# Second attention: one bank and one exponential per transposed score tile, four banks for the other scores, values twice per unit

## What is computed

```python
q = q.reshape(Bx, Sx, N_GROUPS, R, HEAD_DIM).transpose(0, 2, 3, 1, 4)
k = k.reshape(Bx, Sx, N_GROUPS, HEAD_DIM).transpose(0, 2, 1, 3)
v = v.reshape(Bx, Sx, N_GROUPS, HEAD_DIM).transpose(0, 2, 1, 3)
sim = jnp.einsum('bgrsd,bgtd->bgrst', q, k) / math.sqrt(HEAD_DIM)
attn = jax.nn.softmax(sim, axis=-1)
out = jnp.einsum('bgrst,bgtd->bgrsd', attn, v)
```

## Time and profile before

| | |
|---|---|
| median of the runs | 1134.88 us |
| the profiled execution | 1137.65 us, of which the span from first to last instruction is 1135.8 us |
| TensorE (PE) busy | 1015.3 us, 89% |
| VectorE (DVE) busy | 758.1 us, 67% |
| ScalarE (ACT) busy | 592.0 us, 52% |
| stretch of the second attention's units | about 478 to 922 us of the span |

### The profile page before, as it was taken

The page is one execution under the profiler, slowest core; times in us unless marked ns, Lnnn a source line. Parts: engine busy times, 40 slices in busy tenths (PEclk is TensorE's granted clock), DMA queues, the critical chain, the costliest instruction groups (busy, mean ns, idle before and its releaser), DMA issues.

```text
span 1135.8 us, 17286 instructions
## 1 busy us (share of the span) xinstructions
PE 1015.3 (89%) x5701; PEld 744.4 (66%) x5701; DVE 758.1 (67%) x1575; ACT 592.0 (52%) x894; POOL 317.3 (28%) x330
## 2 busy tenths in 40 slices
PE   4999897769999927799998999999999987999996
PEld 3877776669999913555554555555555565888885
DVE  6576544465665436799889888888888846443438
ACT  6324544265555542466665666566656565444431
POOL 2005777065664410000000122222221000455342
PEclk9999999789999969799999999999999998999998
DMA  6862333354444272021121222222222115333244
GB/s 232 326 263 114 112 118 123 104 185 136 132 127 136 98 309 45 7 34 29 26 31 25 44 53 59 58 59 49 64 56 43 63 48 175 107 100 108 89 164 179
DMA packets 48962, 120.20 MB, mean 106 GB/s; under 512 B 7736, under 2 KB 24760, under 8 KB 48344
## 3 DMA queue, kind: packets, MB, share of 16 engines
q1 hardware_dynamic: 35968, 82.67, 25.3%
q0 software_dynamic: 11760, 32.24, 7.5%
q10 hardware_dynamic: 1152, 4.19, 0.9%
HBM read 72.17 MB, written 52.29 MB: 110 GB/s over the span
## 4 chain that ended last, share of the span: by engine, by line
PE 66%; DVE 14%; POOL 7%; ACT 4%; issue 4%; DMA 4%; SPq 0%; ACTq 0%; DVEq 0%; POOLq 0%
PE psum L827 10%; PE psum L849 10%; PE psum L836 8%; POOL xg L475 5%; PE psum L642 5%; PE psum L643 4%; PE psum L644 4%; DVE work_f L1726 4%; PE psum L556 4%; PE psum L557 3%; PE psum L558 3%; PE psum L628 3%; PE psum L653 2%; DVE x L1326 1%; ACT work_f L1219 1%
## 5 line engine op out<-in xcount | busy, mean ns | idle before, releaser
L1726 DVE TENSOR_REDUCE work_f<-psum 128x1 f32<-128x512 f32 x512 | 334.7, 684 | 51.0 <-PE psum L827 49.5
L1219 ACT ACTIVATE work_f<-psum 128x1024 f32<-128x1024 f32 x172 | 168.9, 1023 | 111.9 <-PE psum L836 108.6
L827 PE MATMUL psum<-work_r 128*128 128x512 f32 x512 | 205.0, 439 | 19.9 <-DVE work_f L1726 6.8
L482 POOL DMA_INDIRECT yk<-yb,dest x133 | 129.9, 977 | 241.9 <-ACT yb L1072 213.1
L827 PEld LDWEIGHTS psum<-work_r 128*128 128x128 f32 x512 | 94.2, 190 | 131.3 <-DVE work_f L1726 75.2
L836 PE MATMUL psum<-qm,work_r 128*128 128x512 f32 x512 | 161.9, 398 | 4.2 <-ACT work_f L1219 2.7
L475 POOL DMA_INDIRECT xg<-xn,slot x112 | 108.1, 966 | 180.4 <-PE psum L865 152.2
L836 PEld LDWEIGHTS psum<-qm,work_r 128*128 128x128 f32 x512 | 93.6, 188 | 31.8 <-ACT work_f L1219 10.9
L1219 ACT ACTIVATE pt<-psum 128x1024 f32<-128x1024 f32 x84 | 82.8, 1023 | 50.2 <-PE psum L836 47.6
L642 PE MATMUL psum<-wexp,xbh 128*128 x266 | 103.0, 387 | 6.5 <-issue 5.4
L643 PE MATMUL psum<-wexp,xbh 128*128 x266 | 96.9, 364 | 0.0
(11 more groups left out here) (218 smaller groups left out, 2044.7 us busy)
## 6 DMA issues: line engine op xcount, KB each, us to landing
xb<-xg SPq DMA_DIRECT2D x66, 258.0 KB
xg<-in_pad SPq DMA_DIRECT2D x1, 10320.0 KB
yg<-yk SPq DMA_DIRECT2D x20, 512.0 KB, 9.5
stage<-in_moe SPq DMA_DIRECT2D x16, 608.0 KB
xg<-in_pad SPq DMA_DIRECT2D x1, 7224.0 KB
work_r<-work_r SPq DMA_DIRECT2D x128, 48.0 KB
work_r<-work_r SPq DMA_DIRECT2D x32, 192.0 KB
stage<-in_moe SPq DMA_DIRECT2D x16, 384.0 KB, 3.8
```

What stands on the lines that cost most here:

```text
L482: nc.gpsimd.indirect_dma_start(yk[l], bass.IndirectOffsetOnAxis(ap=dest[:, j % 8, i:i + 1], axis=0), yb[l][:, j % 2, i, :], None).then_inc ...
L827: nc.tensor.matmul(next_bank(pe, ("scores", n), b_mx, n + 1), qs[g % 2][:, t * P:(t + 1) * P], km[g % 4][:, r, :], start=True, stop=True). ...
L1219: nc.scalar.activation(pt[((b * NG + g) * QT + t) % 3][:, 2 * h:2 * h + 2, :], psum[:, 3 + 2 * h:5 + 2 * h, :], ACT.Exp, scale=float(HD) * ...
L1726: v.reduce_max(mx[:, s % 2, i:i + 1], ring["scores", n], AX.X).then_inc(b_mx, 1)
```

## The change

The ring grows to four banks from the 17th use on (banks 3, 2, 0, 1 in turn), so each use waits for the reader of the use four before. The transposed scores get banks 4, 5 and 6, one tile each, and tile m waits for the exponential of tile m-3. ScalarE takes 16 exponentials of 128x512 per unit in place of 8 of 128x1024. The tables put the transposed scores at steps 5 to 16, in ones and twos, and the value tiles two and two at steps 12 and 18, instead of two, one and one at 15, 19 and 25. At step 2 the value tiles now come ahead of the maxima's transposes. The outputs' transposes move from step 11 to 10, the projections from 13 to 8, the values' transposes from 12 to 8; ScalarE's part of `compact` moves from behind the sixth of 8 exponentials to behind the sixth of 16, and its copy of bank 7 to the head of a unit's exponentials.

```diff
-            return {"maxima": 2, "outputs": 11, "values": 12 if s == NG + 1 else never,
-                    "project": 13 if following and NG - 3 <= s < NG else never}
+            return {"maxima": 2, "outputs": 10, "values": 8 if s == NG + 1 else never,
+                    "project": 8 if following and NG - 3 <= s < NG else never}
...
-        ring, read = {}, []
+        ring, holder, uses = {}, {3: (b_va, 1)}, []
 
         def next_bank(engine, use, reader, value):
-            if len(read) >= 3:
-                engine.wait_ge(*read[-3])
-            ring[use] = psum[:, (len(read) + 1) % 3, :]
-            read.append((reader, value))
+            n = len(uses)
+            bank = (n + 1) % 3 if n < QT * R else (3, 2, 0, 1)[n % 4]
+            if bank in holder:
+                engine.wait_ge(*holder[bank])
+            ring[use] = psum[:, bank, :]
+            holder[bank] = (reader, value)
+            uses.append(bank)
             return ring[use]
+
+        def transposed_bank(m):
+            return psum[:, 4 + m % 3, :]
...
             def scores_t(b, g, i):
...
-                t, h = i // 2, i % 2
-                if g >= 1 or i >= 2:
-                    pe.wait_ge(b_ex, b * (2 * NQ) + (g * 2 * QT + i - 1))
-                for r in (2 * h, 2 * h + 1):
-                    ins = nc.tensor.matmul(psum[:, 3 + 2 * h + r % 2, :], km[g % 4][:, r, t * P:(t + 1) * P],
-                                           qm[g % 2], start=True, stop=True)
-                ins.then_inc(b_st, 1)
+                t, r = i // R, i % R
+                m = b * NP + g * QT * R + i
+                if m >= 3:
+                    pe.wait_ge(b_ex, m - 2)
+                nc.tensor.matmul(transposed_bank(m), km[g % 4][:, r, t * P:(t + 1) * P],
+                                 qm[g % 2], start=True, stop=True).then_inc(b_st, 1)
...
-            TRANSPOSED = (4, 5, 8, 11, 12, 13, 16, 17)
-            VALUED = (15, 15, 19, 25)
+            TRANSPOSED = (5, 6, 6, 7, 8, 8, 9, 10, 11, 12, 13, 13, 14, 15, 15, 16)
+            VALUED = (12, 12, 18, 18)
...
-                    if i == turn["maxima"] and back:
-                        maxima_t(b, s - 1)
                     if i == TRANSPOSED[0] and back:
 
                         pe.wait_ge(b_qm, b * NG + s)
                     if s >= 2:
                         follow(b, s - 2, QT * R + i)
+                    if i == turn["maxima"] and back:
+                        maxima_t(b, s - 1)
...
-                        for h in range(2):
-                            if s >= 2 and s % 2 and (t, h) == (1, 1):
+                        tile = (b * NG + s - 1) * QT + t
+                        for r in range(R):
+                            if s >= 2 and s % 2 and (t, r) == (0, 0):
                                 outputs(b, s - 2)
...
+                            if (t, r) == (1, 2) and following and NG - 3 <= s < NG:
+                                compact((0, 2, 1)[s - (NG - 3)], b + 1, ring["projection", b * 3 + s - (NG - 3) + 4], s - (NG - 3))
+                            act.wait_ge(b_st, tile * R + r + 1)
+                            if tile >= 3:
+                                act.wait_ge(b_pv, tile - 2)
+                            nc.scalar.activation(pt[tile % 3][:, r, :], transposed_bank(tile * R + r),
                                                  ACT.Exp, scale=float(HD) ** -0.5).then_inc(b_ex, 1)
-                    if t == 2 and following and NG - 3 <= s < NG:
-                        compact((0, 2, 1)[s - (NG - 3)], b + 1, ring["projection", b * 3 + s - (NG - 3) + 4], s - (NG - 3))
```

More of the change, by code:

```diff
@@ L384, in stack_keys @@
                 else:
-                    sp.wait_ge(b_st, 2 * QT * (u - 3))
+                    sp.wait_ge(b_st, QT * R * (u - 3))
                 for r in range(R):
@@ L806, in _ @@
             pe.wait_ge(m_y, pairs(0, NPAIR[0]))
-            NP, NQ = NG * QT * R, NG * QT
+            NP = NG * QT * R
             def project(n, b1, o):
@@ L830, in scores_t @@
             def scores_t(b, g, i):
-                t, h = i // 2, i % 2
-                if g >= 1 or i >= 2:
-                    pe.wait_ge(b_ex, b * (2 * NQ) + (g * 2 * QT + i - 1))
-                for r in (2 * h, 2 * h + 1):
-                    ins = nc.tensor.matmul(psum[:, 3 + 2 * h + r % 2, :], km[g % 4][:, r, t * P:(t + 1) * P],
-                                           qm[g % 2], start=True, stop=True)
-                ins.then_inc(b_st, 1)
+                t, r = i // R, i % R
[4 more added lines that the diff above has]
+                                 qm[g % 2], start=True, stop=True).then_inc(b_st, 1)
             def values(b, g, t):
-                pe.wait_ge(b_ex, b * (2 * NQ) + ((g * QT + t) * 2 + 2))
+                pe.wait_ge(b_ex, b * NP + (g * QT + t + 1) * R)
                 n = b * NG + g
@@ L866, in maxima_t @@
                 ins.then_inc(b_mt, 1)
-            TRANSPOSED = (4, 5, 8, 11, 12, 13, 16, 17)
-            VALUED = (15, 15, 19, 25)
+            TRANSPOSED = (5, 6, 6, 7, 8, 8, 9, 10, 11, 12, 13, 13, 14, 15, 15, 16)
+            VALUED = (12, 12, 18, 18)
             def follow(b, g, step):
-                for n in range(2 * QT):
+                for n in range(QT * R):
                     if TRANSPOSED[n] == step:
@@ L1211, in stage @@
                     if back:
-                        g = s - 1
-                        for h in range(2):
-                            if s >= 2 and s % 2 and (t, h) == (1, 1):
+                        tile = (b * NG + s - 1) * QT + t
+                        for r in range(R):
+                            if s >= 2 and s % 2 and (t, r) == (0, 0):
                                 outputs(b, s - 2)
[L1216 to L1219, removed]
+                            if (t, r) == (1, 2) and following and NG - 3 <= s < NG:
[4 more added lines that the diff above has]
+                            nc.scalar.activation(pt[tile % 3][:, r, :], transposed_bank(tile * R + r),
                                                  ACT.Exp, scale=float(HD) ** -0.5).then_inc(b_ex, 1)
-                    if t == 2 and following and NG - 3 <= s < NG:
-                        compact((0, 2, 1)[s - (NG - 3)], b + 1, ring["projection", b * 3 + s - (NG - 3) + 4], s - (NG - 3))
                 if last and s == NG:
```

## The result

The changed kernel takes **1145.34 us** (median of 4 runs, 1144.6 to 1146.13), the kernel before 1134.84 us over the same runs: ratio 1.0097, 95% interval 1.0082 to 1.0112, so 9.3 to 12.7 us slower. The forecast was 1136.4 with a range of 1126 to 1149 and "a draw leaning to slower". The profiled execution of the changed kernel took 1146.13 us with a span of 1144.3, 8.5 more than the span before. The profiled execution before lay 2.8 us above its median and this one 0.8, which is why the medians differ by 10.5.

What follows compares the result with a forecast made beforehand. TensorE's streaming time plus stalls was taken to bound each second-attention unit. Plain -1.5, outputs -3.0, projections +8.0, values' transposes -2.6, head -2.3 and tail +2.9 gave +1.5 us on 1134.9: 1136.4, range 1126 to 1149.

Steps and rivals of the forecast that it cites:

- The spacing of single exponentials: On ScalarE: single exponentials follow one another every 0.49 us, with bounds of 0.43 and 0.60.
- the first rival: ScalarE paces the unit, with single exponentials 0.52 to 0.60 us apart: 1142 to 1158 us; chance 26%.
- Increments at no cost: On TensorE: a semaphore increment on each of the 512 transposed scores, before one in two, costs nothing.
- The plain unit: Second attention, unit without extra work: 12.8 us for 12.88, -0.1 per unit, -1.5 over 15 units.
- The three stalls: TensorE in a plain unit: 0.26 us at the first transposed score, 0.27 at number 5, 0.24 at number 14.
- the walk: Step-by-step timing of one changed unit from the end of its second pair of value tiles, giving 12.8 us.
- Units with outputs: Units with the outputs' transposes: four banks hide the division, 13.3 us for 13.52, -0.2 each, -3.0 over 15.
- Projections: Three units per batch: bank wanted again four uses later without value tiles between; 7.5 us per batch, +8.0 over three.
- The third rival: The projection's wait is not paid, hidden by VectorE's and TensorE's backlog: 8 us less, 1128; chance 6%.
- Values' transposes: Unit with the values' transposes: cost falls from 1.36 to 0.44 and some 0.1 us, -2.6 over three batches.
- Head and tail: Before the first double value tile 4.0 us for 6.3, -2.3; after the last 17.1 for 14.2, +2.9.
- two ScalarE pieces per unit in the chain: Sign of being right: chain of waits shows ScalarE pieces of 0.5 to 0.6 us at transposed scores 5 and 14.

Runs made afterwards that it cites:

- one per step: Changed kernel with maxima's transposes ahead of the value tiles, projection at step 11, and transposed scores one per step from step 3: 1118.49 us, ratio 0.9873.

## Why the prediction was right, and what it mis-sized

The direction leaned the right way and the range held, but the forecast of +1.5 us was too small, and 1145.34 lies 9 us above 1136.4. The range reached up to 1149 for the sake of the rival that ScalarE paces the unit, and without that room it would not have held. By its own steps:

- **The spacing of single exponentials**, the unknown on which the first rival hung: 0.49 taken, 0.487 measured. The prediction had the rival decide "from about 0.50 on"; in the trace ScalarE paces half of the transposed scores at 0.49 already. The rival's mechanism was there, without its higher spacing. The length was 0.62, not 0.60, on which little rests. The fixed part and the overlap of an ACTIVATE in the Trainium skill (ScalarE: Activation LUTs, What ACT_TABLE_LOAD costs) give an estimate of 0.52 for the spacing. Eight in 4.03 us do not agree.
- **Increments at no cost**: held. Transposed scores with one each stream at 0.23, and 256 more of them in the old order came with a gain. The Trainium skill (TensorE: Matmul & The Clock Gate, The cost: per-tile semaphore tail) puts 26 ns on each increment where every tile of a group raises one. In this stream of full-array matmuls that is not seen on the path.
- **The plain unit was mis-sized, and this is the step that failed**: 12.8 forecast, 12.99 measured. The three stalls stand where the walk put them: 0.50 for the first transposed score behind the addition, and 0.75 and 0.74 for the pairs. But behind transposed score 5 the walk says "Seven more end at 5.63, score 9 ends at 5.86, just in time for exponential 6 (5.43)". It charged 0.53 from release to result for number 5 alone and let the others stream, although each of them waits for an exponential too. By the walk's own prices number 9 ends at 5.43 + 0.53 = 5.96. Measured, it ends 0.55 us after exponential 6, which is 6.00 after the value block. In the other half, with numbers 13 to 15 paced in the same way, it is 3.29 instead of 3.23. That is 0.2 us in each of 15 plain units and turned -0.1 into +0.1.
- **Units with outputs**: 13.3 forecast, 13.38 measured, where transposed scores are paced as well; the division is hidden as forecast.
- **Projections**: 7.5 us per batch forecast, 7.6 measured, and +8.0 over three was the largest term. The three units grew by 2.36, 2.83 and 2.38 over their kinds where the walk had 2.3, 2.9 and 2.3. Moving the projection took 3.4 per batch back. The third rival did not happen.
- **Values' transposes**: 14.08 - 13.38 = 0.7 instead of 0.5, so -2.0 for -2.6.
- **Head and tail**: first score to first double value tile 42.5 for 44.4 us, -1.9 for -2.3; last double value tile's end to the end 17.4 for 14.2, +3.2 for +2.9 (the seven pieces of the forecast add up to 17.25, not to its 17.1).
- **A sign that did not come**: two ScalarE pieces per unit in the chain. The waits are there, but on the weight loads, and the chain shows them as longer pieces of TensorE.

With the measured unit lengths the sum is 15 x 0.11 - 15 x 0.14 + 8.2 - 2.0 - 1.9 + 3.2 = 7.1 against 7.3 in the traces. Of the 5.6 us that this is above the forecast, 4.0 are the plain units and those with outputs. The medians differ by 10.5. The 3 us between the two are no part of the prediction's mechanism, and their cause stays open: the first score of the profiled executions came anywhere from 436.1 to 444.2 us, in code that none of these kernels changed.

The prediction priced the uncovered addition rightly, at 0.26 us a unit or 8 us in all, and took it for the price of streaming. The runs show that it was a choice: the order of the transposes alone costs 9.5 us of the stretch. Singles are a gain alone (8 us). The fourth ring bank is worth 20.5 us of the stretch in the new order; in the old order, taking it from the transposed scores loses 10. So the losses of the change were the place of the transposes and the place of the projection. Behind them stood a smaller one, of 3.0 us of the stretch: transposed scores in ones and twos, which come closer together than ScalarE takes them.

## What to carry to other kernels

When work is moved in a hand-written order, ask for every result that another engine must return what large block stands between its request and its use; here a 1.85 us block of value tiles covered an addition of 0.70 us, and moving the block ahead of the request uncovered it in all 31 units, while moving a projection away from the block uncovered 1.3 to 1.9 us of ScalarE and 0.7 of VectorE in nine. In a walk, let every matmul that waits for a bank end no earlier than its release plus the restart (0.55 us here), and not only the first of a row: once one of them has waited for an engine that works without a pause, those behind it come at that engine's spacing. A chain counted from end to end can hide this in pieces that look only a little long, so ask what the weight loads waited for. A bank has a value only in an order: count it for each order, and read off who waits for it before giving it to the other side.

## What the runs showed of the hardware that was not expected

A single exponential of 128x512 lasts 619 ns on average (591 to 691), 33 ns longer than a copy of the same shape (586), and still follows the last one after 487 ns. A transposed score that waits for an exponential ends 0.55 us after it; 259 of 512 did in the changed kernel and 29 with one per step. Those that came 0.60 to 0.75 us after it streamed at 0.23, so a near miss costs nothing. And the time ahead of the first score differed by up to 8 us between profiled executions of kernels that are the same up to there. The difference went with the mean granted clock of TensorE between 190 and 290 us of the span, ahead of the change: 0.88 in the six executions with the first score at 436.1 to 437.3, 0.86 in those at 438.5 and 439.6, 0.83 to 0.85 in those at 442.1 and 443.0, and 0.81 in the changed kernel's at 444.2. What lowered it was not tested. So differences of a few us were read from the stretch and from the lengths of plain units and units with outputs, which from the second batch on repeat to 0.05 within a trace.
